# Attention in an order from a list scheduler, with the pieces of the row maxima formed on GpSimd

## The reference, cut to what matters

```python
h = layernorm(x)
q, k, v = h @ Wq, h @ Wk, h @ Wv            # 32 query heads, 8 key/value heads, 16 wide
q, k = rope(q), rope(k)
s = causal_mask(q @ k.T / sqrt(16))         # 1024 x 1024 per head
x = x + layernorm(softmax(s) @ v @ Wo)
x = x + layernorm(moe(layernorm(x)))        # 64 experts, 6 per token, and a shared expert
```

## Time and profile before

| | us |
|---|---|
| median of three runs | 2540.56 (2537.55 to 2584.29) |
| profiled execution | 2544.59 |
| its span, first to last instruction | 2542.5 |

### The profile page before, as it was taken

How to read it: one execution, slowest core, us unless ns; L and a number is a source line. 1 busy time by engine, 2 the same in 40 slices (tenths; PEclk the granted TensorE clock), 3 DMA queues, 4 the chain that set the end, 5 groups by cost and what they waited for, 6 DMA issues and landing times.

```text
span 2542.5 us, 41278 instructions
## 1 busy us (share of the span) xinstructions
PE 2112.5 (83%) x12707; PEld 1004.0 (39%) x12707; DVE 1340.8 (53%) x2959; ACT 1067.3 (42%) x1568; POOL 677.2 (27%) x793
## 2 busy tenths in 40 slices
PE   6899888988999789888997898889978969978840
PEld 3433325544333255443332555333325534444420
DVE  4666644646676356466663564676635512211138
ACT  3455562334555624445555234455552312211100
POOL 2111113631111136311111362111113612222238
PEclk9777789997777889978778999787789989989975
DMA  3112222410000022100000111000001189998988
GB/s 115 43 51 85 85 84 89 150 60 5 10 6 10 10 84 84 41 5 10 10 6 22 56 61 34 5 10 10 9 15 56 61 260 330 332 278 263 277 251 289
DMA packets 108130, 232.81 MB, mean 92 GB/s; under 512 B 24423, under 2 KB 24423, under 8 KB 107920
## 3 DMA queue, kind: packets, MB, share of 16 engines
q1 hardware_dynamic: 81072, 191.07, 22.1%
q0 software_dynamic: 24576, 35.07, 5.7%
q10 hardware_dynamic: 2272, 4.06, 0.4%
HBM read 141.59 MB, written 126.48 MB: 105 GB/s over the span
## 4 chain that ended last, share of the span: by engine, by line
PE 63%; DVE 11%; issue 9%; DMA 7%; ACT 4%; POOL 3%; DVEq 2%; POOLq 1%; SPq 0%; ACTq 0%
PE ps L609 13%; PE ps L539 9%; DVE rmax L1061 6%; DMA gx<-dispatch_scratch 5%; PE ps L496 5%; PE ps L630 5%; PE ps L748 5%; PE ps L695 4%; PE ps L721 3%; PE ps L780 3%; PE ps L734 2%; PE ps L497 2%; PE ps L514 2%; PE ps L546 2%; PE ps L722 2%
## 5 line engine op out<-in xcount | busy, mean ns | idle before, releaser
L1061 DVE TENSOR_REDUCE rmax<-ps 128x1 f32<-128x512 f32 (+3 forms) x1280 | 739.4, 631 | 371.5 <-PE ps L549 220.5
L888 ACT ACTIVATE pr<-ps 128x1024 f32<-128x1024 f32 (+3 forms) x768 | 601.7, 810 | 387.0 <-PE ps L630 383.1
L539 PE MATMUL ps<-kT,qT 48*128 48x512 f16 (+3 forms) x1536 | 467.7, 395 | 59.4 <-DVE rmax L1061 47.5
L609 PE MATMUL ps<-pr,v_ones 128*32 128x512 f32 (+3 forms) x3072 | 412.9, 615 | 45.6 <-ACT raw L878 42.6
L1338 POOL TENSOR_SCALAR_AFFINE_SELECT pr<-pr 128x512 f32<-128x512 f32 x256 | 162.7, 636 | 885.1 <-ACT pr L888 885.1
L630 PE MATMUL ps<-qT,kT 50*128 50x512 f16 (+3 forms) x1536 | 373.4, 383 | 15.9 <-ACT pr L888 9.9
L539 PEld LDWEIGHTS ps<-kT,qT 48*128 48x128 f16 x1536 | 130.2, 102 | 477.1 <-DVE rmax L1061 239.5
L1382 POOL DMA_INDIRECT dispatch_scratch<-x,slot_i x192 | 189.8, 989 | 68.4 <-issue 57.0
L546 PE MATMUL ps<-above,sel 64*128 64x128 bf16 x1024 | 205.3, 248 | 0.0
L748 PE MATMUL ps<-gu_sb,gxT 128*128 128x384 f32 x512 | 201.8, 520 | 0.0
L1401 POOL DMA_INDIRECT acc_scratch<-eo,etok x64 | 98.6, 1541 | 315.6 <-DVE eo L1215 265.2
(11 more groups left out here) (148 smaller groups left out, 2564.5 us busy)
## 6 DMA issues: line engine op xcount, KB each, us to landing
gu_sb<-w_gu_dram SPq DMA_DIRECT2D x64, 768.0 KB, 6.5
dn_sb<-w_dn_dram SPq DMA_DIRECT2D x64, 384.0 KB, 8.9
dispatch_scratch<-blank SPq DMA_DIRECT2D x8, 2308.0 KB, 8.1
gx<-dispatch_scratch SPq DMA_DIRECT2D x64, 288.5 KB, 5.3
xin<-x_dram SPq DMA_DIRECT2D x32, 256.0 KB, 2.7
acc_scratch<-blank SPq DMA_DIRECT2D x32, 256.0 KB, 2.1
xres<-x_dram SPq DMA_DIRECT2D x32, 256.0 KB, 3.3
x_scratch<-x SPq DMA_DIRECT2D x32, 256.0 KB, 2.0
```

Of the source, the lines that this page charges most:

```text
L539: last = pe.matmul(o, qT[r:r + SROWS, half, 2 * g + h // 2, q % QPH * P:(q % QPH + 1) * P], kT[r:r + SROWS, g, kh * HALF:kh * HALF + w], s ...
L609: last = pe.matmul(ps[32 * h:32 * h + 32, 6, c0:HALF], v_ones[g % 2][:, kt, :], pr[i % SLOTS][:, h, 0:HALF - c0], start=kt == 0, stop=kt = ...
L888: act.activation(pr[i % SLOTS][:, 2 * pair:2 * pair + 2, 0:HALF - c0], ps[:, 2 + 2 * pair:4 + 2 * pair, 0:HALF - c0], ACT.Exp, scale=facto ...
L1061: dve.tensor_reduce(dst[:, heads[0] % 2, heads[0] // 2:heads[0] // 2 + n, q % QPH], ps[:, BANK_OF[item], 0:n * w].rearrange("p (h k) -> p ...
```

## The change

`spread`, `group_items`, `LAG` and the fixed group loops go. In their place the source runs a list scheduler, `plan_attention`, when the program is built. It keeps a clock for PE, ACT, DVE and POOL, gives each operation a fixed duration and each hand-over a latency, and always appends to PE's list the operation that could start first (the head of each of four queues: stack transposes, units or maxima, S, P); ACT's and POOL's lists come out of the same run. The program then issues exactly these lists. The last tile's stack transposes join them (in bank 6, one after another), the first stage ends one step earlier, and only part of group 0's units stay in it. Two neighbouring units may be issued together, their matmuls alternating between the two halves of PE's rows. `t1` moves from behind the second unit of the next group to behind the fourth, `t0` from behind unit 19 to behind unit 21. `finish_half` moves from DVE to POOL, as three operations on 128x16 with two drains between them; DVE keeps only the joining of the two parts.

```diff
-LAG = 2
-def group_items(g):
-def item_cost(g, item):
-def spread(g):
+def stream_items():
+    items = [("u", 0, u) for q in range(LAST_Q - 1, TT) for u in range(NU) if UNITS[u][1] == q]
+    for g in range(KVH):
+        follow = [("u", g + 1, u) for u in range(NU)] if g + 1 < KVH else []
+        if follow:
+            follow.insert(NU0 + 10, ("t0", g + 1))
+        follow.insert(min(4, len(follow)) if g else 0, ("t1", g))
+        items += follow
+    return items
+def plan_attention():
+    LAT, DRAIN, ROWS = 0.06, 0.17, 2.1
...
+    while stq or pvq or ring or stackq:
+        follow()
+        choices = []
...
+        if ring:
+            item = ring[0]
+            at = max(now["pe"], bank_free(item))
+            if item[0] == "u":
+                at = max(at, can_score(item))
+                if len(ring) > 1 and ring[1][0] == "u" and item[2] % 2 == 0:
+                    choices.append((max(at, bank_free(ring[1])), 1, "two"))
+                choices.append((at, 2, "one"))
+            else:
+                choices.append((max(at, most.get(item, FAR) + LAT), 1, "max"))
...
+            choices.append((at, 3, "st"))
...
+            choices.append((at, 4, "pv"))
+        at, _, what = min(choices)
...
+        elif what == "st":
+            now["pe"] = at + (HALF - PUNITS[key[1]][2]) / 2400 + 0.006
...
+            now["pe"] = at + 0.18 + (HALF - PUNITS[key[1]][2]) / 600 + 0.01
...
@@ PE
+                for what in PE_ORDER:
+                    if what[0] == "stack":
+                        stack_transpose(TT - 1, what[1])
+                    elif what[0] == "st":
+                        scores_transposed(*what[1:])
+                    elif what[0] == "pv":
+                        outputs(*what[1:])
+                    else:
+                        ring(what[1])
@@ DVE, reduce_unit
+                    if item[1] and item[2] in (0, NU0):
+                        dve.wait_ge(max_ready, 2 * (KVH * b + item[1]) - 1 + (item[2] == NU0))
...
-                    if item[2] == NU0 - 1:
-                        finish_half(item[1], 0)
                     if item[2] == NU - 1:
-                        finish_half(item[1], 1)
+                        dve.drain()
+                        dve.tensor_tensor(rmax[:, 16:32], rmax[:, 16:32], rmax[:, 32:48], ALU.max).then_inc(parts_joined, 1)
@@ POOL
+                def finish_half(g, half):
+                    gg = KVH * b + g
+                    if half == 0:
+                        wait_apart(pool, sc_reduced, PER_BATCH * b + RANK["u", g, NU0 - 1] + 1)
+                    else:
+                        wait_apart(pool, parts_joined, gg + 1)
+                    m = rmax[:, 16 * half:16 * half + 16]
+                    if g > 0:
+                        wait_apart(pool, maxT_done, 2 * gg + half - 1)
+                    pool.tensor_scalar(nm[:], m, -1.0 / ONE, None, ALU.mult)
+                    pool.drain()
+                    pool.tensor_copy(mb[half][:, 0:16], nm[:])
+                    pool.drain()
+                    pool.tensor_tensor(mb[half][:, 16:32], nm[:], mb[half][:, 0:16], ALU.subtract).then_inc(max_ready, 1)
```

More of the change, by code:

```diff
@@ L70, in early_plan @@
     plan = []
-    for step in range(3, TT + 2):
+    for step in range(3, TT + 1):
         if step == TT:
             plan.append((step, ("t0", 0)))
-        plan += [(step, ("u", 0, u)) for u in range(NU) if UNITS[u][1] == step - 3]
-    return plan
-def group_items(g):
[L80 to L88, removed]
@@ L91, in item_cost @@
-def item_cost(g, item):
[L93 to L98, removed]
-def spread(g):
[L103 to L117, removed]
+        units = [("u", 0, u) for u in range(NU) if UNITS[u][1] == step - 3]
@@ new lines, in early_plan @@
+        if step == TT:
+            units = EARLIER[4:] + units
+        if step == TT - 1:
+            EARLIER.extend(units)
+            units = units[:4]
+        plan += [(step, item) for item in units]
+    return plan
+def stream_items():
[7 more added lines that the diff above has]
+    return items
@@ L559, in ring @@
                 def ring(items):
-                    items = list(items)
-                    while items:
-                        item = items.pop(0)
+                    for item in items:
                         free_bank(item)
[L565 to L575, removed]
+                        if item[0] == "u" and item[1] == 0:
+                            pe.wait_ge(stack_copied, 3 * (TT * b + UNITS[item[2]][1] + 1))
+                    if items[0][0] == "u":
+                        score_units(items)
+                    else:
+                        max_transpose(items[0], BANK_OF[items[0]])
                 x_transpose(0)
-                for s in range(TT + 2):
+                for s in range(TT + 1):
                     early = [item for step, item in EARLY if step == s]
@@ L612, in outputs, with scores_transposed @@
                     last.then_inc(pv_done, 1)
-                def group(g):
+                def scores_transposed(g, i, pair):
                     gg = KVH * b + g
[L616 to L643, removed]
+                    qh, kt, c0 = PUNITS[i]
+                    if i == 0 and pair == 0:
+                        pe.wait_ge(max_rows[0], 64 * (gg + 1))
+                    if i == HALF1 and pair == 0:
+                        pe.wait_ge(max_rows[1], 64 * (gg + 1))
+                    if i >= 1 or g >= 1:
+                        pe.wait_ge(exp_done, 2 * NP * gg + 2 * i + pair - 1)
+                    elif pair == 0:
+                        pe.wait_ge(qkv_read, TT * (b + 1))
+                    else:
+                        pe.wait_ge(stack_copied, 3 * TT * (b + 1) - 3)
@@ L1347, in _ @@
                 copy_v(1)
-                for g in range(KVH):
-                    group(g)
+                for what in POOL_ORDER:
+                    if what[0] == "mask":
+                        mask(*what[1:])
+                    elif what[0] == "fin":
+                        finish_half(*what[1:])
+                    else:
+                        wait_apart(pool, pv_done, NP * (KVH * b + what[1] - 1))
+                        copy_v(what[1])
                 end_phase(pool, b, 0)
```

276 lines of the change are left out of this document (207 added, 69 removed).

## The result

The changed kernel took **2384.51 us**, median of 4 runs (2361.80 to 2411.14), beside 2558.93 for the kernel before on the same chip: a ratio of **0.936, interval 0.922 to 0.950**. Ratios here compare only the executions within 1.5% of their kernel's fastest, so they differ somewhat from the ratio of two medians over all. Measured again later in more rounds it stood at 0.942 (0.933 to 0.950), some 147 us. The forecast was 2328, with a range of 2275 to 2500; the time lies where the first rival put it (2392, a low stretch half as long). The profiled execution took 2411.14 us, 133 less than the profiled one of before.

The account below looks back on a forecast made before the run. DVE was taken to bound a period's first part, half-clock PE the second, with a 24.4 us floor. Gains of 6 x 6.6 + 10 + 5 = 54.6 us a batch, 218 in four, gave 2328 us, range 2275 to 2500.

Parts of the forecast that it names:

- the first rival: Attention periods: the clock still falls once each; half a low stretch 29.4 us, 2392 (chance 0.22), full 32.1, 2472 (0.14).
- What bounds the kernel: Attention period of 34.1 us: DVE bounds the first part, slow PE the second; floor is PE's 24.4 us at full clock.
- The even order: Attention period without the burst of five units: PE 90% busy at full clock, 24.4/0.90 = 27.2 us.
- The new wait: Before S g.4, PE stops some 1.5 us a group for t1's row stores; net 0.3 us added, period 27.5.
- the clock holds: Attention periods: clock stays up with PE kept fed, period 27.5 us, kernel 2275 to 2370 us; chance 0.42.
- The pieces on POOL: Maxima pieces in each half: about 1.1 us on POOL, some 0.9 us off DVE per period; counted at nothing.
- Units in twos: Ring units issued in pairs may overlap on two halves of PE's rows; counted at nothing.
- Head: Start of each batch's attention, 92 to 131.4 us: overlap and a dropped step gain 10 us, between 0 and 17.
- Tail: End of each batch's attention, 335.9 to 384.2 us: clock held gives up to 6 us, little after; 5 taken.
- The sum: All attention: 6 x 6.6 + 10 + 5 = 54.6 us a batch, four times 218, giving 2328 us.

Follow-up runs that it names:

- rows35: Changed kernel with the planner's time for the t1 row stores set to 3.5 us instead of 2.1; 2306.10 us, again (rows35_again) 2311.67 us, ratio 0.913.
- norows1: Changed kernel, lists untouched, without the row stores of t1, so no maxima are subtracted in the second half; 2305.13 us, ratio 0.915 to the kernel before.
- oldpool: Kernel before with its order of PE and ACT untouched, but the pieces of the maxima formed on POOL; 2522.79 us, ratio 1.001.
- newdve: Changed kernel, lists untouched, but the pieces of the maxima formed on DVE as before; 2416.83 us, ratio 0.961 to the kernel before.
- split: Changed kernel, lists untouched, but paired units issued one after the other; 2360.76 us, ratio 0.937 to the kernel before.
- t0early: Changed kernel with 3.5 us planned for the row stores, and t0 of group 0 one first-stage step earlier; 2308.07 us, ratio 0.906 to the kernel before.
- rows48head: Changed kernel with 4.8 us planned for the row stores, and t1 of group 0 behind four units of group 1; 2324.60 us, ratio 0.933.
- rows0: Changed kernel with the planner's time for the t1 row stores set to 0 instead of 2.1 us; median 2401.36 us.

## Why the prediction was off, step by step

**What bounds the kernel: right.** PE's work at full clock was put at 24.4 us a period from the row of before. Once nothing stops it, PE is busy 24.41 and 24.82 us in periods of 25.1 and 25.2. DVE's 23 and ACT's 20 held too.

**The even order, counted at 24.4/0.90 = 27.2: too dear.** I took the 90% from the best stretch of the old order. The new one keeps PE 97% busy where the clock is up, and 97 and 98% in the two periods of rows35_again. This step erred by some 2 us a period towards slow.

**The new wait, "Net I add 0.3": the step that failed.** Its time was right: 5.2 us predicted from transpose to rows, 5.36 measured; a pause of 1.5, 1.3 to 1.9 measured, at the place named. What I didn't follow was its effect on the clock. I netted the pause against waits that go away, and put a fall of the clock into a rival as if it were independent of it. But the pause brings the fall with it in nearly every group: where the pause goes, in norows1 and in rows35, nearly all low stretches of these periods go too. On average a period is 28.9 us with it and 25.4 to 25.5 without, so it costs 3.4 us a period (4 in those shown) and not 0.3; by maxima time 78 to 84 us in all. The two errors partly cancel in the period: 27.5 predicted, 28.9 measured on average and 29.7 over the six of batch 0. That the forecast lies only 2 to 3% below the result is in part this luck.

**The likeliest case, "the clock holds": wrong; the first rival, half a low stretch: right** in its sign, its place and its size (period 29.4 against 28.9 to 29.7; 2392 against 2384.51). Its "for" had named S g.4. I weighed against it that the clock did not fall in the last 17 us of a period at 90% busy; but the pauses that the trace of before names in there are of 0.31, 0.92 and 0.35 us. The longest:

```profile
295.58 1.07 PE L609 MATMUL ps<-pr,v_ones 128*32 128x512 f32 x8 [0.92 <-ACT raw L878]
```

None is like a pause of 1.9, and that was in reach. But the length of the longest pause isn't the whole measure either: the fall of before near 271 follows no pause over 0.35 us, only the burst, in which PE is busy 2.75 of 3.80 us in short pieces; and oldpool has 20 pauses of 1.04 to 1.49 us without a fall within 5 us. What decides is not shown. The rule (the Trainium skill, TensorE: Matmul & The Clock Gate, section "What's actually happening") that activity releases the throttle is borne out only in part here: PE is busy 6.80 of 6.80 us at 0.50 first.

**The pieces on POOL: size right, worth wrong.** The chain on POOL was put at 1.1 us and took 0.95: 0.25, 0.20 and 0.22 with what lies between. Only the subtraction has two inputs: 0.220 us on POOL against 0.176 on DVE, 1.25 times as long, less than the factor of two that the Trainium skill gives for two inputs (GPSIMD Engine Reference, section "Engine selection"). The prediction applied that factor to DVE's 0.175, which is the multiplication, with one input; on POOL it takes 0.253, 1.45 times as long. The prediction also added the PEld and the PE row of waits for pieces, which are the same 32 transposes: PE waited 21.0 us and not 48, 0.66 at each t1 and nothing for pieces at t0. The cover holds in every group but the first, where t1.0 waits:

```profile
120.03 0.29 PE L718 MATMUL ps<-id_h,mb 128*32 128x128 f16 x1 [2.20 <-POOL mb L1472]
```

PE's waits for pieces go from 21.0 us to 9.5, but the order does that, since newdve has 7.0. I counted the move at nothing; by newdve against after it is worth some 20 to 25 us (maxima time 935.1 to 912.7) in the new order, most likely by banks that come free sooner, and nothing by the ratio in the old one (oldpool).

**Units in twos, counted at nothing: right** (split).

**Head, 10 us: nothing came.** The clock of the head is 0.58 to 0.70 in all versions, 0.65 before and 0.61 after. The copy of t0.0 comes 5.7 us earlier (94.3 for 100.0), but that of t1.0 comes at 120.35 for 117.10. I had seen the serial chain and still counted half of the room. **Tail, 5 us: more came.** From the end of the six periods to the first transpose of the output stage it is 36.4 us (309.3 to 345.7) against 48.3 (335.9 to 384.2 in the earlier trace rows), 11.9 less. Together 12 for 15.

**The sum.** 54.6 us a batch predicted. Measured in batch 0, 384.2 to 345.7: 38.5, of which 26.6 in the six periods and 11.9 around them. Four times 38.5 is 154; the last copy gained 142. Of the 16 us a batch that are missing, 13 are in the periods (39.6 predicted).

**Open.** Why the head stays low: PE is busy 31.9 of 39.4 us there with the clock at 0.61, and 33.2 at 0.65 in norows1. t0early and rows48head changed its order and not its clock. And why the low stretch lasts 6.8 us in one group and 10.2 or 3.4 in the next, or 13.7 and 3.4 in batches of oldpool, at the same order of work. No run takes away the burst of units alone, so how the order's 100 us divide between the burst, the distances and the rest is open.

## What to carry to other kernels

A pause of PE in a dense stretch is to be priced with the low clock behind it, not by its own length: here 1.3 to 1.9 us of waiting cost 3 to 4 us a period. In a list scheduled in the source the due time of a DMA chain must be the measured one, issue and landing together (4.8 us here, not 2.1); too large a number costs little as long as there is other work to put in (846.4 us of maxima time at 4.8 against 834.6 at 3.5). Moving small work to an idle engine lengthens its chain and pays where the order leaves that chain room; what it gave here came most likely from the engine that it left, not from the chain.

## What was not expected of the hardware

- PE at 0.50 did not get its clock back for 6.8 us after, 100% busy, for 13.3 before, 97% busy, and from about 99 to 130 us in the head, with pauses.
- A pause of 2.80 us in rows0 brought no fall of the clock, while pauses of 1.3 to 1.9 us after brought one in 22 of 24 cases.
- The same instructions in the same order went with low stretches of 13.7 us in three batches of oldpool and of 3.4 us in most of the fourth: periods of 34.1 and 30.7 us.
- Four stores of one small tile take SP 3.04 us to issue, nearly twice the 1.70 us of the landing: the queue, not the transfer, is most of the row stores.
- Work that is the same in all kernels, behind attention, took 620 to 696 us between executions, a spread of about half of what this change is worth.
